# Three convolutions and a local attention in one pass: the low halves of the second convolution's inputs are formed on GpSimd in place of VectorE

## The reference

```python
q = jnp.einsum('bhwd,de->bhwe', x, Q_P)
k = jnp.einsum('bhwkd,de->bhwke', stk, K_P)      # stk: the 9 neighbours of each point
v = jnp.einsum('bhwkd,de->bhwke', stk, V_P)
scores = jnp.einsum('bhwke,bhwe->bhwk', k, q) * mask
alpha = jax.nn.softmax(scores, axis=-1)
t = x + jnp.einsum('bhwk,bhwke->bhwe', alpha, v)
t_in = t
t = jax.nn.relu(_conv(t, ff1_kernel, ff1_bias))
t = jax.nn.relu(_conv(t, ff2_kernel, ff2_bias))
t = jax.nn.relu(_conv(t, ff3_kernel, ff3_bias))
return t_in + t
```

## Time and profile before

| | before |
|---|---|
| median of three runs | 2083.73 us (2083.67 to 2085.44) |
| the profiled execution | 2084.2 us |
| its span, first to last instruction | 2082.4 us |
| mean granted TensorE clock | 0.992 |
| ScalarE busy | 1088.4 us (52%) |
| DMA, mean busy share of the 16 engines | about 5 tenths |

### The profile page before, as it was taken

One profiled execution on the slowest core, in us unless ns is written; L12 is line 12 of the kernel. 1 busy time (PEld: TensorE's weight loads), 2 busy tenths in 40 slices (PEclk: granted clock), 3 DMA queues, 4 the chain that ended last, 5 costly groups with the idle time before them and its releaser, 6 DMA issues.

```text
span 2082.4 us, 61988 instructions
## 1 busy us (share of the span) xinstructions
PE 2025.3 (97%) x23866; PEld 1240.9 (60%) x23866; DVE 1815.4 (87%) x2502; ACT 1088.4 (52%) x3086; POOL 17.2 (1%) x28
## 2 busy tenths in 40 slices
PE   4899999999999999999999999999999999999997
PEld 3566656656665655655656655665656665665554
DVE  3699899899899899899889899899888989989986
ACT  3464555555555555555555455455455455455422
POOL 3000000000000000000000000000000000000000
PEclk9899999999999999999999999999999999999999
DMA  5555555555555555555555554554555555554532
GB/s 146 124 149 170 164 143 171 156 148 167 155 152 167 155 157 158 157 163 150 160 158 155 161 168 141 165 167 140 166 165 141 170 162 144 168 166 144 155 128 86
DMA packets 286054, 320.89 MB, mean 154 GB/s; under 512 B 87802, under 2 KB 220218, under 8 KB 279482
## 3 DMA queue, kind: packets, MB, share of 16 engines
q1 hardware_dynamic: 285982, 319.92, 53.0%
HBM read 150.23 MB, written 33.82 MB: 88 GB/s over the span
## 4 chain that ended last, share of the span: by engine, by line
PE 96%; DVE 2%; ACT 1%; issue 1%; DMA 0%; SPq 0%; DVEq 0%; ACTq 0%
PE conv_banks L502 32%; PE conv_banks L462 16%; PE conv_banks L527 13%; PE side_banks L527 13%; PE side_banks L443 6%; PE side_banks L422 4%; PE conv_banks L402 4%; PE side_banks L431 3%; PE side_banks L453 3%; PE side_banks L414 2%; ACT prob L724 1%; DMA xs<-x_bands 0%; DVE work L962 0%; DVE deven L882 0%; DVE deven L883 0%
## 5 line engine op out<-in xcount | busy, mean ns | idle before, releaser
L502 PE MATMUL conv_banks<-dodd,w3f 128*64 128x512 f32 (+2 forms) x1616 | 491.4, 581 | 11.0 <-DVE work L929 9.3
L502 PE MATMUL conv_banks<-deven,w3f 128*64 128x512 f32 (+2 forms) x1616 | 490.3, 579 | 0.0
L724 ACT ACTIVATE prob<-side_banks,negmax 128x100 f32<-128x100 f32 x1024 | 344.9, 378 | 162.5 <-DVE negmax L847 162.5
L462 PE MATMUL conv_banks<-dt,w1f 128*64 128x256 f32 (+2 forms) x4128 | 377.6, 378 | 0.0
L462 PEld LDWEIGHTS conv_banks<-dt,w1f 128*64 128x64 f32 (+1 forms) x4128 | 233.7, 135 | 121.0 <-issue 42.1
L502 PEld LDWEIGHTS conv_banks<-dodd,w3f 128*64 128x64 f32 x1616 | 148.3, 137 | 245.4 <-issue 219.7
L724 ACT ACTIVATION_READ_ACCUMULATOR prob<-side_banks,negmax 128x1 f32 x1024 | 246.9, 241 | 0.0
L502 PEld LDWEIGHTS conv_banks<-deven,w3f 128*64 128x64 f32 x1616 | 152.8, 137 | 143.1 <-issue 139.7
L736 ACT COPY rq<-conv_banks 128x512 f32<-128x512 f32 x128 | 68.7, 589 | 305.2 <-PE conv_banks L402 305.2
L962 DVE TENSOR_TENSOR work<-side_banks,work 128x1024 f32<-128x1024 f32 (+1 forms) x130 | 154.4, 1230 | 78.6 <-PE side_banks L527 78.6
L741 ACT COPY probt<-side_banks 100x1024 f32<-100x1024 f32 x128 | 130.2, 1017 | 157.2 <-PE side_banks L431 157.2
(11 more groups left out here) (92 smaller groups left out, 3282.5 us busy)
## 6 DMA issues: line engine op xcount, KB each, us to landing
xk<-x_keys SPq DMA_DIRECT2D x65, 800.0 KB
xc<-x_bands SPq DMA_DIRECT2D x65, 650.0 KB, 4.8
xr<-x_bands SPq DMA_DIRECT2D x260, 128.0 KB, 2.9
dodd<-dodd SPq DMA_DIRECT2D x65, 512.0 KB, 5.6
out<-work SPq DMA_DIRECT2D x64, 512.0 KB, 4.1
xs<-x_bands SPq DMA_DIRECT2D x130, 128.0 KB, 3.1
dt<-dt SPq DMA_DIRECT2D x65, 256.0 KB, 4.8
deven<-deven SPq DMA_DIRECT2D x65, 256.0 KB, 6.1
```

Source lines behind the costliest of these rows:

```text
L462: mm = nc.tensor.matmul(bank[(LOWER, UPPER)[o], n * 256 + lo * 64:n * 256 + hi * 64], w1f[i][rows, m, s, o * C:o * C + C], dt[rows, lo + s ...
L502: mm = nc.tensor.matmul(bank[rows, lo_ * 128:hi_ * 128], w3f[:, m, s, odd * C:odd * C + C], source[:, lo_ + s // 2:hi_ + s // 2, m], start ...
L724: last = nc.scalar.activation(prob[:, g, a], score_banks[g // 2][:, g % 2, a * KEYS:(a + 1) * KEYS], ACT.Exp, bias=negmax[:, g, a:a + 1], ...
```

## The change

`u_low` leaves VectorE's program and becomes a program of its own on GpSimd, which runs through the same steps by `schedule`, with the two calls of a step right behind one another. The arithmetic and the tiles stay the same. Since GpSimd is not in order with VectorE, VectorE now waits before it writes new `du` (`inputs`, part 0) until both parts of the step before have been read, and for that the semaphore `du_low` starts from 2, by one more memset on `credits`. TensorE's waits on `du_low` count from there.

```diff
             def go_on2(G, k, j, ahead=None):
 
-                pe.wait_ge(du_low, G * 2 + (j // 2 + 1))
+                pe.wait_ge(du_low, parts(G, j // 2))
                 for s in range(2):
...
-            def u_low(G, k, part):
-                dve.wait_ge(du_high, G * 2 + (part + 1))
-                streams, n = PARTS[part], new_slots(CONV1, k)
-                nc.vector.tensor_tensor(dul[:, 1:n + 1, streams], du[:, 0:n, streams],
-                                        duh[:, 1:n + 1, streams].bitcast(F32), ALU.subtract).then_inc(du_low, 1)
-
...
                 if part == 0:
                     dve.wait_ge(relu_done, relus(G, which, behind))
-                    if which != CONV1:
+                    if which == CONV1:
+                        dve.wait_ge(du_low, parts(G, 1, 1))
+                    else:
                         dve.wait_ge(v_kept, G * 32 + (32 - 32 * behind))
...
                 if att == ASK:
                     scale(b + 2, 0)
-                u_low(G, k, 0)
                 if att == ASK:
                     scale(b + 2, 1)
                 outer3(G, k)
-                u_low(G, k, 1)
                 finish(G, k, b)
...
-                    (d_done[EVEN], 2), (sent, 32), (t_kept, 16), (u_kept, 32), (pool_zeroed, 1))):
+                    (d_done[EVEN], 2), (sent, 32), (t_kept, 16), (u_kept, 32), (du_low, 2), (pool_zeroed, 1))):
                 nc.gpsimd.memset(credits[:, i:i + 1], 0.0).then_inc(credit, n)
             pool.wait_ge(w3_in, 16)
             whole_weights(nc.gpsimd, pool.wait_ge, raws[3], w3f, half3, w3_stage).then_inc(w_ready, 1)
+
+            def u_low(G, k, part):
+                pool.wait_ge(du_high, G * 2 + (part + 1))
+                streams, n = PARTS[part], new_slots(CONV1, k)
+                nc.gpsimd.tensor_tensor(dul[:, 1:n + 1, streams], du[:, 0:n, streams],
+                                        duh[:, 1:n + 1, streams].bitcast(F32), ALU.subtract).then_inc(du_low, 1)
+
+            def step(G, p, k, b, par, att):
+                u_low(G, k, 0)
+                u_low(G, k, 1)
+
+            schedule(pool, step)
```

## The result

The changed kernel takes 2094.8 us (median of five runs, 2094.09 to 2096.97) beside 2084.44 for five runs of the kernel before; the ratio is 1.0051, with a 95% interval of 1.0037 to 1.0066. Its profiled execution, the slowest of the five, has a span of 2095.0 us, 12.6 more than before.

The account below looks back on a forecast made before the run. TensorE's own work was taken as the bound, so relieving VectorE gains 0 and regular steps cost 0. Seven steps' stalls, 11.3 us, brought the profiled 2084.2 to 2095.5, 2095 as a median; range 2082 to 2183.

Parts of the forecast that it names:

- TensorE bounds, relief is worth nothing: TensorE busy all 31.00 us of a step, so VectorE's freed 2.44 us gains 0; rival of relief, 2079 us, 0.05.
- GpSimd's duration: One 128x1024 subtraction on GpSimd was taken at 2.38 us, with an upper bound of 2.77.
- The handovers of 0.08: A waiting GpSimd instruction starts some 0.08 us after its releaser; used for every handover.
- GpSimd first in every step: Rival: above 2.61 us GpSimd's part 1 precedes the second product in 53 regular steps too; 2179 to 2189 us, chance 0.23.
- The product is held to GpSimd's end and 0.85 more: Softmax product on VectorE, two SBUF inputs, waits for GpSimd's subtraction to end, then needs 0.85 us; rival not held, 0.34.
- Who comes first: Second product against GpSimd's part 1: VectorE first by 0.23 us in 53 regular steps, GpSimd first in seven.
- The price: Seven steps with an earlier second cast stall TensorE: three by 1.43 us, four by 1.75, sum 11.3 us.

Follow-up runs that it names:

- part 1 alone on GpSimd: Changed kernel with part 0 of `u_low` back on VectorE between the scales, part 1 staying on GpSimd: 2084.01 us, 0.9997 of the kernel before.
- the multiplication: Changed kernel with GpSimd's subtraction replaced by `du` times 0.5, one input, low halves left out: 2083.52 us, 0.9999.
- The two memset kernels: Changed kernel plus one VectorE memset between the two scales, of 128x320 or 128x160: 2163.99 us (1.0379) and 2096.15 us (1.0056).
- the order was changed: Changed kernel with GpSimd also waiting for the second scaled half of the probabilities before part 1: 2087.92 us, 1.0013 of the kernel before.
- the memset of 128x160: Changed kernel plus one VectorE memset of 128x160 between the two scales, delaying the second product: 2096.15 us, 1.0056.
- its copy: Changed kernel with GpSimd's subtraction replaced by a copy of `du`, one input, low halves left out: 2084.12 us in one run.

## Why the prediction was right

**TensorE bounds, relief is worth nothing.** Right. The kernel with part 1 alone on GpSimd takes 1.22 us a step from VectorE and is at 0.9997. The trace has a gain where part 1 left VectorE's queue, in two steps of the tail, 0.22 and 0.23 us, and none in a regular step.

**GpSimd's duration.** Taken at 2.38, measured 2.36 to 2.38 undisturbed. The handovers of 0.08 were 0.08. The whole of "GpSimd first in every step" hung on this term: it needed 2.61.

**The product is held to GpSimd's end and 0.85 more.** This was the assumption with the least behind it, since the earlier trace rows shows a hold for other instructions only. It holds: 526.01 + 0.85 = 526.86. The rule cited from the Trainium skill ("SBUF — State Buffer", § Who interferes with whom) agrees with these runs on which pairs meet: two SBUF inputs against a GpSimd instruction that reads (2.89 and 1.68 us in place of 0.99), but not against one that only writes (0.99), and not with an operand in PSUM (`outer3`, 1.29). Where it has the pair held for the whole instruction, the multiplication differs: about 1.03 of 2.77 us.

**Who comes first.** I had VectorE ahead by 0.23 us in regular steps, and GpSimd ahead by 0.11 in step 16 and 0.16 in step 17. Measured 0.24 (527.01 against 527.25), 0.11 and 0.14 (622.89 against 623.03). The two memset kernels show that the whole effect turns on this order.

**The price.** 1.43 us for step 16 was 1.29 (33.94 - 32.65), 1.75 for step 17 was 1.76 (31.99 - 30.23); over the seven, 10.8 by the ends of the first casts beside 11.3. That the medians came so close, 2094.8 against 2095, is in part luck: the kernel before had 2084.44 in this comparison and not the 2083.73 that the sum starts from, and the difference was 10.4. Within the sum one piece was left out and did not show. The prediction held the first product against a deadline in the regular step alone (1022.68, 3.58 us behind the first cast's end); in step 17 the matmuls that need it start at 2.71, and the 0.7 us lost there were covered by the later and larger stall for `outer3`. It came out when the order was changed, 3.5 to 3.6 us in place of the 1.7 expected.

**What I had not in the sum.** The span of the profiled execution is 12.6 us over the one before, not 11.3. The difference lies at the two ends. The start was 0.45 us shorter, two steps of the tail gained 0.44, and in the last two steps it lost 2.56: TensorE starts at the low clock behind its gap of 4.46 us, and stays on it for longer. The first 6 us behind that gap, before and after (the number in front of the last two is the granted clock):

```profile
2054.07:2060.07 6.00, 6.00 (x22) 1.95 (x24) 2.57 (x8) 2.13 (x5) 0.00 (x0) 0.77 0.00 0
```

```profile
2064.07:2070.07 6.00, 6.00 (x14) 1.72 (x16) 2.58 (x8) 1.49 (x4) 0.00 (x0) 0.50 0.00 0
```

Before, the clock was back at 2.4 GHz during these 6 us; after, it was at 1.2 GHz for all of them, and once more from 2083.7 to 2087.0, a stretch that the kernel before doesn't have. These runs do not make it a price of the change. The kernel with the memset of 128x160 has the same seven late steps (10.75 us) and the same gap of 4.46 us, but 0.72 of the clock in the 6 us behind it; it loses 0.33 us there, and its span is 10.6 us over the one before. The medians of the changed kernel differ by 10.4 as well. What decides between the short and the long stretch stays open.

## What to carry to other kernels

An elementwise instruction moved to GpSimd is priced by what it holds on VectorE, not by VectorE's idle time: list the VectorE instructions with two SBUF inputs that can fall beside it, and ask for each pair who starts first and when the held one is needed. Put the order into the program, as a margin of 0.1 us that falls out of the schedule was worth 68 us here; but look where the hold goes next, since behind a wait it went to `finish` and 3 us stayed. The only arrangement without a cost left part 0 on VectorE, between the products, and none of those tried was faster than the kernel before. VectorE, busy at 87% and not the bound, gave nothing back in a regular step when it was relieved, but became late where it was held.

## What the runs showed of the hardware that I had not expected

- GpSimd's multiplication of 128x1024 held VectorE's product for about 1.03 of its 2.77 us (if the product needs 0.85 once it is free, as behind the other two), its copy for all of 1.04, its subtraction for all of 2.37.
- The hold goes both ways within a step: beside a product that started 0.24 us earlier the subtraction took 3.01 in place of 2.36, held by 0.65 us of the 0.75 that the product still ran.
- A wait on TensorE in front of a matmul that would have started 0.42 us ahead of the end of the matmul before it costs that overlap as well: in step 17, 0.73 us late with only 0.35 us of idle time in the timeline.
